# Cross attention's value products: eight heads per visit every fourth slot, and a ring of six exponential tiles

## The reference

```python
h = layernorm(x + multihead(x, x, x, sa_wq, sa_wk, sa_wv, sa_wo, causal=True), ln1_g, ln1_b)
h = layernorm(h + multihead(h, encoding, encoding, ca_wq, ca_wk, ca_wv, ca_wo, causal=False), ln2_g, ln2_b)
ff = jax.nn.relu(h @ ff_w1.T + ff_b1) @ ff_w2.T + ff_b2
return layernorm(h + ff, ln3_g, ln3_b)
# multihead, with dh = 16 channels per head and scale = 16:
scores = jnp.einsum('bqhd,bkhd->bhqk', q, k)
att = jax.nn.softmax(scores / scale, axis=-1)
out = jnp.einsum('bhqk,bkhd->bqhd', att, v).reshape(B, Sq, D)
```

## Time and profile before

| | |
|---|---|
| median of three runs | 875.87 us |
| profiled execution | 875.57 us, span 873.8 us |
| PE busy | 787.0 us, 90% of the span |
| VectorE (DVE) busy | 659.1 us, 75% |
| ScalarE (ACT) busy | 438.0 us, 50% |
| GpSimd (POOL) busy | 485.5 us, 56% |
| mean granted TensorE clock | 0.96 of full speed |
| cross attention's value products (line 963) | 512 matmul records from 389.5 to 702.2 us, 43.4 us busy |

### The profile page before, as it was taken

The page is one execution under the profiler, slowest core; times in us unless marked ns, Lnnn a source line. Parts: engine busy times, 40 slices in busy tenths (PEclk is TensorE's granted clock), DMA queues, the critical chain, the costliest instruction groups (busy, mean ns, idle before and its releaser), DMA issues.

```text
span 873.8 us, 19903 instructions
## 1 busy us (share of the span) xinstructions
PE 787.0 (90%) x7214; PEld 651.1 (75%) x7232; DVE 659.1 (75%) x1498; ACT 438.0 (50%) x907; POOL 485.5 (56%) x598
## 2 busy tenths in 40 slices
PE   5896799999999898788789999999999889999895
PEld 4665677777777675555468888888877789989784
DVE  3545767777777989677989999998888776867863
ACT  4431355555565565556555555555544544444442
POOL 2401466677666676554345666666555775657541
PEclk9999999999999999899789999999999999999987
DMA  8397588768765765346432222222200020012122
GB/s 269 60 356 189 108 132 140 139 118 128 131 115 111 115 105 102 76 88 121 79 72 53 54 52 53 53 53 53 53 2 10 2 77 2 28 54 81 54 81 76
DMA packets 105296, 79.58 MB, mean 91 GB/s; under 512 B 43255, under 2 KB 101961, under 8 KB 104941
## 3 DMA queue, kind: packets, MB, share of 16 engines
q1 hardware_dynamic: 101434, 72.02, 39.9%
q10 hardware_dynamic: 3764, 6.29, 2.0%
HBM read 27.03 MB, written 12.97 MB: 46 GB/s over the span
## 4 chain that ended last, share of the span: by engine, by line
PE 61%; DVE 18%; issue 6%; ACT 3%; SPq 1%; DMA 1%; POOL 1%; POOLq 0%; DVEq 0%; ACTq 0%
PE a_misc L87 14%; PE a_pair L87 11%; PE a_s L1002 8%; PE a_pair L963 3%; PE a_pair L791 3%; PE a_s L767 3%; PE a_pair L948 3%; PE a_pair L809 3%; PE a_s L765 2%; PE a_s L87 2%; PE a_s L925 2%; PE a_pair L1101 2%; DVE a_rest L1420 2%; ACT a_parts L1139 2%; DVE c_z L1509 1%
## 5 line engine op out<-in xcount | busy, mean ns | idle before, releaser
L1405 DVE TENSOR_REDUCE a_nm<-a_s 128x2 f32<-128x512 f32 (+1 forms) x192 | 127.5, 680 | 54.9 <-PE a_s L767 53.3
L1912 POOL TENSOR_TENSOR c_hidden<-c_hid,c_hidden 128x256 fp32r<-128x256 f32 x128 | 95.8, 748 | 118.3 <-DVE c_hid L1647 118.2
L1168 ACT ACTIVATE a_pT<-a_pair 128x512 f32<-128x512 f32 x192 | 113.8, 597 | 93.8 <-PE a_pair L791 87.4
L1263 ACT ACTIVATE a_pT<-a_pair 77x512 f32<-77x512 f32 x128 | 75.9, 593 | 141.9 <-PE a_pair L948 137.5
L1002 PE MATMUL a_s<-c_w,c_hidden 128*128 128x256 f32 x768 | 118.6, 294 | 0.0
L87 PE MATMUL a_pair<-c_fxh,c_w 128*128 128x256 f32 x512 | 101.5, 291 | 12.8 <-DVE c_hid L1647 12.8
L1819 POOL TENSOR_SCALAR_AFFINE_SELECT a_pT<-a_pT 128x256 f32<-128x256 f32 (+1 forms) x192 | 91.1, 492 | 30.2 <-ACT a_pT L1168 29.9
L1002 PEld LDWEIGHTS a_s<-c_w,c_hidden 128*128 128x128 f32 x768 | 99.9, 192 | 0.7 <-issue 0.4
L87 PEld LDWEIGHTS a_pair<-c_fxh,c_w 128*128 128x128 f32 x512 | 80.0, 193 | 15.8 <-DVE c_hid L1647 15.6
L791 PE MATMUL a_pair<-a_sq,a_sk 98*128 98x256 bf16 (+1 forms) x512 | 76.0, 252 | 7.3 <-ACT a_pT L1168 7.1
L1647 DVE TENSOR_SCALAR c_hid<-a_pair,ff_b_col 128x256 f32<-128x256 f32 x128 | 61.3, 479 | 28.0 <-ACT c_hidden L1289 27.9
(11 more groups left out here) (255 smaller groups left out, 2141.2 us busy)
## 6 DMA issues: line engine op xcount, KB each, us to landing
a_sq<-a_parts SPq DMA_DIRECT2D x96, 128.0 KB, 4.4
a_sk<-a_parts SPq DMA_DIRECT2D x96, 128.0 KB, 4.4
a_sq<-c_parts SPq DMA_DIRECT2D x96, 128.0 KB
x<-in_xT SPq DMA_DIRECT2D x16, 256.0 KB, 5.9
res<-in_x SPq DMA_DIRECT2D x16, 256.0 KB, 5.6
out<-g_fin SPq DMA_DIRECT2D x16, 256.0 KB, 2.1
a_sk<-kc_parts SPq DMA_DIRECT2D x96, 38.5 KB
fold_rows<-x_fold ACTq DMA_DIRECT2D x1, 2496.0 KB, 11.3
```

The lines of the kernel that those rows point to most:

```text
L1168: nc.scalar.activation(pT[g % NPT][:], stps[g % 2][:], ACT.Exp).then_inc(s_exp, 1)
L1263: nc.scalar.activation(pT[g % NPX][0:SC], st_ps[0:SC, :], ACT.Exp).then_inc(c_exp, 1)
L1405: nc.vector.tensor_reduce(nm[c % 2][:, QT * heads[0] + qt:QT * heads[-1] + qt + 1:QT], sps[g % 2][:].rearrange("p (h k) -> p h k", h=len(h ...
L1912: nc.gpsimd.tensor_tensor(hl(m), hid[n % NHID][:], f32(hh(m)), ALU.subtract).then_inc(c_hl, 1)
```

## The change

A visit now treats eight heads, in every fourth slot: the visits of slots 1 and 5 go, and those of slots 3 and 7 do their heads too. CAV_LAG goes from 13 to 15, so that the merged visit stands where the second of the two stood. The ring of exponential tiles grows to six. The two new tiles lie in two pieces each, in gaps between other tensors (`split_tile`): the view has two halves of 256 columns at a fixed distance. ScalarE now writes, and PE reads, all six through such a view. The sixth tile's first write waits for the end of the causal part (`s_st`). `c_av` is still raised twice per eight heads, by the last matmul of each half.

```diff
-    NPT, NVP, NPX, NHID = 6, 4, 4, 3
+    NPT, NVP, NPX, NHID = 6, 4, 6, 3
-    CST_LAG, CAV_LAG, UP_LAG = 11, 13, 44
+    CST_LAG, CAV_LAG, UP_LAG = 11, 15, 44
...
+    split_tile = lambda n, place, off, step: at(n, [P, 2, step // 4], F32, place, off)[0:SC, :, 0:S]
+    xpT = [v[0:SC].rearrange("p (h q) -> p h q", h=2) for v in pT[0:4]]
+    xpT += [split_tile("pT4", "a_parts0", 5 * 4 * S, t.place["a_parts1"] - t.place["a_parts0"]),
+            split_tile("pT5", "a_sk2", 5 * 2 * S, t.place["a_sk3"] - t.place["a_sk2"])]
...
-            def cross_values(rr):
-                c, r = divmod(rr, 4)
+            def cross_values(p):
+                c, j = divmod(p, 2)
                 if not real(c):
                     return
-                ro = r % 2
-                pe.wait_ge(c_exp, 2 * rr + 2)
-                if rr == 0:
+                pe.wait_ge(c_exp, 4 * p + 4)
+                if p == 0:
                     pe.wait_ge(s_tr, 2 * B - 1)
-                if ro == 0:
-                    atleast(pe, c_tr, rr // 2)
-                for i in range(4):
-                    last = mt(av_ps[32 * i:32 * i + 32, ro * S:ro * S + S], vc[c % NSTK][:, 4 * r + i, :],
-                              pT[(2 * rr + i // 2) % NPX][0:SC, i % 2 * S:i % 2 * S + S], start=True, stop=True, skip_group_check=True)
-                last.then_inc(c_av, 1)
+                atleast(pe, c_tr, p)
+                for ro in range(2):
+                    for i in range(4):
+                        last = mt(av_ps[32 * i:32 * i + 32, ro * S:ro * S + S], vc[c % NSTK][:, 8 * j + 4 * ro + i, :],
+                                  xpT[(4 * p + 2 * ro + i // 2) % NPX][:, i % 2, :], start=True, stop=True, skip_group_check=True)
+                    last.then_inc(c_av, 1)
...
-                if (g - CAV_LAG) % 2 == 0:
-                    cross_values((g - CAV_LAG) // 2)
+                if (g - CAV_LAG) % 4 == 0:
+                    cross_values((g - CAV_LAG) // 4)
...
-                if g < NPX:
+                if g < 4:
                     act.wait_ge(s_av, (NU - NPT + g) // 3 + 1)
+                if g == 5:
+                    act.wait_ge(s_st, NU)
                 atleast(act, c_av, (g - NPX) // 2 + 1)
-                nc.scalar.activation(pT[g % NPX][0:SC], st_ps[0:SC, :], ACT.Exp).then_inc(c_exp, 1)
+                nc.scalar.activation(xpT[g % NPX], st_ps[0:SC, :].rearrange("p (h q) -> p h q", h=2), ACT.Exp).then_inc(c_exp, 1)
```

## The result

| | before | after |
|---|---|---|
| median of four runs each | 875.6 us (874.03 to 876.85) | 888.46 us (883.7 to 889.19) |
| ratio, with its 95% interval | | 1.013 [1.0106, 1.0154] |
| profiled execution | 875.57 us, span 873.8 | 887.91 us, span 886.1 |
| mean granted TensorE clock of it | 0.964 | 0.953 |

The changed kernel is slower, by 1.3%. The forecast was 880.3 us with a range of 872.0 to 884.5, so the direction was right and the size was not: the loss is 12.6 us by the forecast's own base and not 4.4. The same kernel in two later comparisons gave ratios of 1.0135 [1.0109, 1.0162] and 1.0102 [1.0068, 1.0137]. All ratios and means leave out executions more than 1.5% above the fastest of their kernel and group.

The account below looks back on a forecast made before the run. PE, busy 90% of the span, was taken to bound the kernel. Turns 7, 8, 9, 11, 12 (1.8), 13 to 17 (2.2) and 1 to 4 (0.4) add 4.4 us to 875.87: 880.3 us, range 872 to 884.5.

Parts of the forecast that it names:

- A visit's price: PE's visits: one removed frees 0.66 us, four more heads cost about 0.43, so a merge wins 0.23, 32 merges 7.3.
- The floor before the projection: Turns 7, 8, 9, 11, 12: the path to the output projection cannot go below 15.27 us; 0.37 us longer each, 1.8 together.
- Turns 6 and 10 at nothing: Turns 6 and 10: PE already waits there, so slot 3's added work disappears in the waits: 0 us.
- Turns 13 to 17 at 0.43 each: Turns 13 to 17: PE waits for DVE, nothing is won and slot 3's 0.43 us is paid in full: 2.2 us.
- A pause of 0.6 to 0.8 us before the projection and one of 0.1 us in slot 7: Signs in turns 7 to 12: PE pauses before the output projection, and waits for DVE's hidden in slot 7.
- The first turns at +0.4 us: Turns 1 to 4: added work partly vanishes in PE's waits; +0.4 us, between bounds of -2 and +3.
- turn 5 at nothing: Turn 5: slot 5 already waits 0.63 us for maxima, so the added work costs 0 us.
- Rival D: A moved wait changes whether the clock falls; one stretch more or less costs or gives up to 4 us; chance 0.07.
- The 0.8 us of new idle time in each turn: Middle turns: PE's idle time rises by 0.83 us while its busy time falls by 0.46, making a turn 0.37 longer.

Follow-up runs that it names:

- the projection moved: Changed kernel with the output projection of slot 2 issued behind the down and up tiles instead of in front: 871.95 us, ratio 0.996.
- filling the early pauses: Changed kernel with the first half of each merged visit of turns 1 to 5 issued once more where the small visit stood: 887.22 us, ratio 1.0137.
- the added matmuls: Changed kernel with two more matmuls on constants ahead of the output projection in turns 14 to 16: 882.87 us, ratio 1.0075; again 884.37 us, ratio 1.0101.

## Why the prediction was wrong

Step by step, as the prediction put it.

- **A visit's price** (1.21 us for eight heads, 32 visits of 16 records): measured 1.21 in the visit looked at. With the projection moved, the turn fell by 0.34 us of the 0.46 that two merges are worth by this price. The drain at a change of tiling mode, of which the Trainium skill speaks (TensorEngine Tiling (Array Packing), Key Properties), shows in the trace as far as it can be read there: 0.20 us to the first matmul of the merged visit (516.52 - 516.32), where a step without a change of mode is 0.12. The merge does save it, 32 times; it was the rest of the schedule that couldn't use it.
- **The floor before the projection** (0.07 us won, 0.43 paid, 0.37 a turn): right in its place and nearly in its size, with 0.28 to 0.34 measured in turns 7, 8, 9, 11 and 12, in sum 1.49 us against 1.8. The path from turned scores to projection was shortened by 0.16 us and not 0.07 (517.72 to 532.90 is 15.18 us; the floor was put at 15.27), as the end of DVE's small operation comes a little nearer.
- **Turns 6 and 10 at nothing**: -0.58 and -0.02 measured. **Turns 13 to 17 at 0.43 each**: 0.41 to 0.44 in four of them and 0.28 in the last. Turn 6 to turn 17 are 2.9 us in sum, where the forecast had 4.0. This part of the mechanism was right and its size somewhat too large.
- **A pause of 0.6 to 0.8 us before the projection and one of 0.1 us in slot 7**: both are there. The first is 0.6 us by the starts (0.75 from the turned scores, where 0.14 was usual), the second 0.13.
- **The first turns at +0.4 us** is the first step that failed, and with it turn 5 at nothing. The bound was -2 to +3, and its lower end does not follow from its own words (seven removed visits at 0.66 us are 4.6). Turns 2 to 5 cost 2.6 to 3.4 us in most profiles and 6.2 in the one of the first comparison; by timing the early part cost 1.2 and 4.4 us in two groups, 2.6 us over 17 executions. The sum was made as if a changed wait only shifted work at the clock that the row before showed. In these turns the kernel before already stood at 1.2 GHz for 20.4 us, and with merged visits it was 23.8 or 30.6. How much of the loss is the clock and how much the waits was not taken apart.
- **Rival D** is the second, and the larger one in the first comparison. It allowed one stretch more or less, up to 4 us, with a chance of 0.07, and looked for it in the first turns alone. What came were three short stretches in turns 10 to 17 at 1.5 us each, where the kernel before had none, and the earlier fall in turn 2. In the first comparison's profile that is 6.2 us in turns 2 to 5, 2.9 by the schedule from turn 6 on and 4.5 by the three stretches, less the 0.9 us by which its turn 2 started earlier. The 0.8 us of new idle time in each turn is a number of the prediction's own; it was counted as lost time, and the clock was left as it was.

So the means divide as follows. Merged visits from turn 6 on cost 4.4 us (880.0 against 875.6). The schedule alone is 2.9 of that by the profile without a stretch, and one stretch per execution would be the rest; the forecast's 4.0, which had no stretch in it, came near 4.4 by luck. The first turns cost 2.6 us. Both together cost 10.0 over the eleven later executions, and 11.9 in the first comparison's four. What is over, 3.0 us with a standard error of 1.2, goes with 11 us more at the lower clock than the parts bring (14.4 against 2.1 and 1.2). Within one kernel, an execution is 0.26 us longer for each us more at 1.2 GHz (the 101 of before) or 0.32 (the eleven of after), by which 11 us more are 2.9 to 3.5 us of time. That agrees in size, and so would two stretches more per execution. The Trainium skill (TensorE: Matmul & The Clock Gate, its table of terms) puts the penalty at the throttled time times what is missing from the full clock, here half. By that rule the 14.4 us more at 1.2 GHz would be 7.2 us, an estimate. The slopes within one kernel show less, 3.7 to 4.6 us; that part of such a stretch lies where PE waits for DVE anyway would explain it and was not tested.

**What stays open.** That the changed kernel spends more time at 1.2 GHz than before is measured (83.4 against 69.0 us, standard errors 2.6 and 0.6). In turns 2 to 5 it goes with the merged visits in sixteen profiles of seventeen. That the new pauses bring it is argued and not shown. Against it: the same pause was followed by a fall in one kernel and by none in another, and filling the early pauses changed nothing. In turns 14 to 16 no run filled the pauses, since the added matmuls came behind them; the mean went from 83.4 to 73.8 us with them, yet both profiled executions kept their stretches there, and in the one group with both kernels the medians differ by 1.3 us with intervals that overlap. Whether the surplus over the two parts is real is open too: 3.0 us over all groups, 0.6 in the group that had all three, or 1.7 there with the execution of 890.95 us.

## What to carry to other kernels

Before matmuls are taken from a full PE, find the next instruction on PE that waits for another engine and how long ago it was released: if that is a small part of the saving (0.17 of 0.66 us at the projection here), the saving stops there, and independent work that stands behind the wait should be moved in front of it together with the change. Here that turned a loss of 10 us into a gain of 3 to 4. And where a change turns PE's work into pauses, give the clock a term with a width of its own: a stretch in a full turn cost 1.5 us here, one kernel drew none to three of them in turns 10 to 17, and the range should hold several.

## What the runs showed of the hardware

- The same binary draws a different number of stretches at 1.2 GHz from execution to execution. Three profiles of one kernel had three, one and none in turns 10 to 17, and its 31 executions lie between 875.2 and 889.2 us, 1.6% apart, with mean granted clocks of 0.949 to 0.967. By that spread a ratio of 0.5% needs some ten executions of each kernel, an estimate. The Trainium skill (TensorE: Matmul & The Clock Gate, Part 1) says of the ramp at a kernel's start that the number of slow matmuls varies between runs and that it costs under 1% of a typical span. The draws here lie in the middle of the kernel, and were as large as the change.
- A small DVE operation on two columns (line 1987) took 0.56 to 1.24 us in the twelve turns of the kernel before in which it met POOL's o_low, and ended 0.02 us after it each time; beside an idle POOL it took 0.15. Its neighbours `a_var` (line 1968) and `a_root` (line 1970) were held in the same way by other POOL operations. The batch norm aggregations, on two columns as well, kept their 0.18 us beside POOL. In the kernel after it is the same. That this keeps DVE from using scores that come earlier is read from the timeline; no run took the meeting away.
